# One transfer in place of four for each stored tile of dt and dt*x, and one in place of three for the rows of maxima

## The chip, the cores and the metric

The kernel runs on one core of one Trainium2 chip. The metric is the device time of one execution in microseconds (us). Before the change it is 4890.47 us, the median of three runs from 4883.07 to 4906.68 us.

## What is computed

The reference takes `L0_attn_hidden_states`, 16 sequences of 512 positions and 256 features, and passes each through six residual layers:

```
x = x + 0.5 * _L0_ffn_ref(_layernorm(x), ...)     # gated FFN, 704 wide, inputs and weights quantised in blocks of 16
x = x + _L0_attn_ref(_layernorm(x), ...)          # a state space layer ("Mamba")
x = x + 0.5 * _L0_ffn_ref(_layernorm(x), ...)
x = x + 0.5 * _L1_ffn_ref(_layernorm(x), ...)     # linear layer with 8 routed low-rank experts
x = x + _L1_attn_ref(_layernorm(x), ...)          # causal attention, 16 heads of 16, ALiBi bias
x = x + 0.5 * _L1_ffn_ref(_layernorm(x), ...)
```

Two of them matter here. The state space layer has 512 channels and 16 states per channel:

```
dt = softplus(dt_low @ W_dt + b_dt)
h  = exp(dt_t[..., None] * A) * h + (dt_t * x_t)[..., None] * B_t[:, None, :]
y  = einsum('bds,bs->bd', h, C_t)
```

The attention layer takes a softmax over scores from which the maximum of each row is subtracted first.

## The kernel before

**The stages.** Each of the 16 sequences passes through a "front" FFN, a "head" (the projections of the state space layer: convolution, dt, dt*x and the gate z), a "scan" (16 rounds of the recurrence), a "back" FFN, a first "lora" stage, "attention" and a second "lora" stage. Different sequences are in different stages at one time. On every engine a fixed table of due times (`PE_PLAN`, `DVE_PLAN`, `ACT_PLAN`, `POOL_PLAN`, `SP_PLAN`, with a period of 261.461 us) merges the stages into one list of instructions. An engine works its list off in order. So one wait holds back everything behind it on that engine, whatever stage it belongs to.

**The stores of the head.** In the head the channels are worked on in four tiles c = 0 to 3 of 128 channels by 512 positions. For each tile VectorE (DVE) writes dt (lines 1556 to 1562) and dt*x (1567), and sets the first column of dt to zero (1569). SyncE (SP) waits for that last step and issues the stores to `dt_scratch` and `dtx_scratch` in DRAM (line 572). A tile is 128 rows of 2 KB. It is stored with channels interleaved, so that later one group of four channels can be read as one run of 8 KB: in DRAM, channel 32 j + m stands in row 4 m + j. Before, that is written as four transfers of 32 rows each, one for each j. The SBUF buffers `dt` and `dtx` hold two tiles each, so tiles 0 and 2 share a buffer, and tiles 1 and 3 the other.

**Who waits for these stores.** Each buffer has a semaphore (`dt_saved[0]`, `dt_saved[1]`, the same for `dtx_saved`). These wait for them:

- ScalarE (ACT) at line 878, before it writes tile c >= 2 of dt (line 879), for the store of tile c - 2;
- DVE at line 1566, before it writes tile c >= 2 of dt*x, for the store of tile c - 2;
- DVE at line 1574, before the gate's tile m = 0 or 1 (line 1577), which takes the place of dt in the same buffer, for the store of tile 2 or 3;
- SP at lines 609 and 610, before the first load of the four rounds that read tile c;
- ACT at lines 802 and 818, before later stages write over the same memory.

TensorE's products for the gate (line 1149) wait in turn for line 1577, which frees the PSUM bank.

**The loads of the scan.** For each of 16 rounds SP issues two loads of 1024 KB, `decay` (line 616) and `state` (622). Each reads 8 rows of 8 KB and repeats each for 16 partitions. All transfers of the kernel are issued by SP on one queue.

**The rows of maxima.** In attention ACT copies the maxima, split in three bf16 parts, to `m_rows`: 12 partitions, that is 3 parts of 4 heads, of 512 elements (line 959). SP copies them into three single partitions of `qh` (line 665): one transfer for each part, 4 KB each. TensorE's scores (line 1310) wait for them, and so does the next write of `m_rows` (line 958).

Of the kernel before, what the change touches and what calls it, by code (L numbers as in the profile page):

```python
# [28 lines left out]
G = 4  # L29
J = H // G  # L30
# [6 lines left out]
Q = 4  # L37
# [48 lines left out]
def build(nc, a, out):  # L86
    with ExitStack() as ctx:
# [422 lines left out]
        def _(eng):  # L510
# [49 lines left out]
            def head(i):  # L560
                yield 31
                eng.wait_ge(head_dve.sem, head_dve.after(i, f"silu{C - 1}"))
                eng.dma_start(xs_scratch[i], xs).then_inc(xs_saved, 16)
                yield 33
                eng.wait_ge(head_act.sem, head_act.after(i, "pj"))
                eng.dma_start(bc_scratch[i], pj[RK + 1:, :]).then_inc(bc_saved, 16)
                for c in range(C):
                    yield 40 + 2.8 * c
                    eng.wait_ge(head_dve.sem, head_dve.after(i, f"zero{c}"))
                    for src, dst, done in ((dt, dt_scratch, dt_saved), (dtx_of(i), dtx_scratch, dtx_saved)):  # L570
                        for j in range(Q):
                            eng.dma_start(dst[i, c].rearrange("(q e j) l -> j (q e) l", q=Q, j=Q)[j], src[32 * j:32 * (j + 1), c % 2, :]
                                          ).then_inc(done[c % 2], 16)
                for m in range(C):
                    yield 53.7 + 2 * m
                    eng.wait_ge(head_dve.sem, head_dve.after(i, f"siluz{m}"))
                    eng.dma_start(gz_scratch[i, m], gz[:, m % 2, :]).then_inc(gz_saved[m % 2], 16)

            def scan(i):
# [23 lines left out]
                for r in range(ROUNDS):  # L603
# [4 lines left out]
                    if r % Q == 0:  # L608
                        eng.wait_ge(dt_saved[c % 2], 64 * (2 * i + c // 2 + 1))
                        eng.wait_ge(dtx_saved[c % 2], 64 * (2 * i + c // 2 + 1))  # L610

# [27 lines left out]
            def attention(r, q):  # L639
# [22 lines left out]
                def load_maxima(j):  # L662
                    eng.wait_ge(att_act.sem, att_act.after(r, f"m{j}"))
                    for w in range(3):
                        eng.dma_start(qh[MAXROW + w:MAXROW + w + 1, j % 2, :, :], m_rows[w * G:(w + 1) * G, :]).then_inc(m_loaded, 16)

# [77 lines left out]
        def _(eng):  # L744
# [52 lines left out]
            def lead(w, n, norm, q):  # L797
                p = WORK.index((w, n))
                if p >= 2 and WORK[p - 2][0] == "head":
                    yield 4.9  # L800
                    for saved in dtx_saved:
                        eng.wait_ge(saved, 128 * (WORK[p - 2][1] + 1))
                yield from hats(norm, q, xx[:, n % NX, :, :])
                if w != "head":
                    yield 10.5
                    r = FFNS.index((w, n))
                    eng.wait_ge(f.lead_dve.sem, f.lead_dve.after(r, "scaled"))
                    eng.activation(size_x[:, :], norm.hat[:, :, :].rearrange("p t d -> p (t d)"), ACT.Abs, scale=BINADE
                                   ).then_inc(f.lead_act.sem, f.lead_act.step("size"))

            def ffn(front, r, n):
# [3 lines left out]
                if heads:  # L815
                    eng.wait_ge(xs_saved, 16 * heads)
                    for b in range(2):
                        eng.wait_ge(dt_saved[b], 128 * heads)
                        eng.wait_ge(gz_saved[b], 32 * heads)
# [35 lines left out]
            def head(i):  # L855
# [18 lines left out]
                for c in range(C):  # L874
                    yield 35 + 2.8 * c
                    eng.wait_ge(head_pe.sem, head_pe.after(i, f"dt{c}"))
                    if c >= 2:
                        eng.wait_ge(dt_saved[c % 2], 64 * (2 * i + 1))
                    eng.activation(dt[:, c % 2, :], MB[(1 + c) % 2][:, :], ACT.Abs).then_inc(head_act.sem, head_act.step(f"abs{c}"))
# [57 lines left out]
            def attention(r, q):  # L937
# [16 lines left out]
                def save_maxima(j):  # L954
                    eng.wait_ge(att_pe.sem, att_pe.after(r, f"m{j}"))

                    if j or r:
                        eng.wait_ge(m_loaded, 48 * (J * r + j))
                    eng.activation(m_rows[:, :], att_bank[f"m{j}"][0:3 * G, :], ACT.Copy).then_inc(att_act.sem, att_act.step(f"m{j}"))
# [44 lines left out]
        def _(eng):  # L1004
# [243 lines left out]
            def attention(r, q):  # L1248
# [46 lines left out]
                def scores(w, j, t, g, n):  # L1295
# [4 lines left out]
                    if t == 0 and g == 0:  # L1300
                        if w == "s":
                            eng.wait_ge(qk_loaded[b], SET_LOADS * (2 * r + j // 2 + 1))
                        else:
                            eng.wait_ge(m_loaded, 48 * (J * r + j + 1))
                    for h in range(n):
# [80 lines left out]
        def _(eng):  # L1386
# [118 lines left out]
            def ffn(front, r, n):  # L1505
                small = [f.qs[:, n, :] for n in range(4)]

                def hidden(t):
                    for p, (lo, width) in enumerate(PIECES):
                        yield 21.2 + p + TILE_US * t  # L1510
                        heads = heads_before(r)
                        if t == 0 and p == 0 and heads:
                            eng.wait_ge(xs_saved, 16 * heads)
                            for b in range(2):
                                eng.wait_ge(dt_saved[b], 128 * heads)
                                eng.wait_ge(gz_saved[b], 32 * heads)
# [20 lines left out]
            def head(i):  # L1537
# [14 lines left out]
                for c in range(C):  # L1552
# [12 lines left out]
                    if c >= 2:  # L1565
                        eng.wait_ge(dtx_saved[b], 64 * (2 * i + 1))
                    eng.tensor_tensor(dtx_of(i)[:, b, :], dt[:, b, :], xs[:, c, :], ALU.mult).then_inc(head_dve.sem, head_dve.step(f"dtx{c}"))
                    eng.wait_ge(head_dve.sem, head_dve.after(i, f"dtx{c}"))
                    eng.memset(dt[:, b, 0:1], 0.0).then_inc(head_dve.sem, head_dve.step(f"zero{c}"))
                for m in range(C):  # L1570
                    yield 52.5 + 2 * m
                    eng.wait_ge(head_act.sem, head_act.after(i, f"tanhz{m}"))
                    if m < 2:
                        eng.wait_ge(dt_saved[m], 128 * (i + 1))
                    else:
# [185 lines left out]
```

## Time and profile before

| | |
|---|---|
| median of three runs | 4890.47 us |
| profiled execution, from its first to its last instruction (span) | 4905.3 us |
| PE (TensorE matmul) busy | 4033.8 us, 82% |
| DVE busy | 3994.1 us, 81% |
| ACT busy | 2371.7 us, 48% |
| POOL (GpSimd) busy | 1600.0 us, 33% |
| SP's DMA queue, time of its packets as a share of 16 engines | 64.9% |
| read from and written to HBM | 647.30 MB, 101.71 MB |

For the profiled execution the record has the span alone, with no time around it. The span is 14.8 us (0.3%) above the median of the runs and within their range. "SPq" in a row is SP's issuing of a transfer. The chain of waits is followed back from the last instruction: each piece is what released the piece after it, so the pieces fill the span. A piece "DMA a<-b" lasts from the end of the issue (or from the start of the last one) to the moment at which the waiting engine is released. A landing time is counted from issue to completion.

### The profile page before, as it was taken

What the parts mean: (1) busy time and instruction counts of PE and PEld (TensorE: products, weight loads), DVE (VectorE), ACT (ScalarE), POOL (GpSimd) and SP (SyncE); (2) the same over time, 40 slices, a digit from 0 to 9 for tenths busy, and PEclk for the clock granted to TensorE, in tenths of its full rate; (3) what the DMA queues carried; (4) which work ended last, traced back from release to release, by engine and by line L of the source; (5) the groups of instructions that cost most, each with busy time, mean ns of one, the idle gap of its engine ahead of it and who ended that gap; (6) DMA issues with size and microseconds to landing.
All of it is one profiled execution on the core that took longest, in us unless ns stands there. A gap on an engine that the chain in (4) does not pass through costs nothing.

```text
span 4905.3 us, 54168 instructions
## 1 busy us (share of the span) xinstructions
PE 4033.8 (82%) x18222; PEld 2046.2 (42%) x18251; DVE 3994.1 (81%) x5964; ACT 2371.7 (48%) x4341; POOL 1600.0 (33%) x1036
## 2 busy tenths in 40 slices
PE   4556678888989898888989898988989898786867
PEld 2223334443535354444435354444435353434343
DVE  6578889898989989898989889898989899684402
ACT  2334344555555464645555554646555554543322
POOL 0143433333334333333333333333333343332000
PEclk8778889999999999999999999999999999897867
DMA  1477668767676777777677777787677777772100
GB/s 56 118 176 180 149 170 182 174 158 185 159 171 175 163 177 175 180 166 178 158 177 178 157 176 159 177 179 180 156 176 173 159 176 161 181 174 64 42 23 28
DMA packets 241433, 753.39 MB, mean 154 GB/s; under 512 B 37650, under 2 KB 132659, under 8 KB 171524
## 3 DMA queue, kind: packets, MB, share of 16 engines
q1 hardware_dynamic: 241156, 749.95, 64.9%
q8 instruction: 144, 2.36, 0.2%
q14 instruction: 133, 1.09, 0.1%
HBM read 647.30 MB, written 101.71 MB: 153 GB/s over the span
## 4 chain that ended last, share of the span: by engine, by line
PE 47%; DVE 23%; ACT 11%; DMA 9%; issue 4%; SPq 3%; POOL 2%; ACTq 0%; DVEq 0%; POOLq 0%
PE m L1135 8%; DVE state L1608 5%; PE m L1107 5%; DVE mt L1696 4%; DMA decay<-dt_scratch 4%; DMA state<-dtx_scratch 3%; PE y L1212 2%; PE pd L1334 2%; PE m L1149 2%; DVE u L1603 2%; PE y L1201 2%; DMA dt_scratch<-front 2%; ACT shared L982 2%; PE m L1136 1%; ACT decay L912 1%
## 5 line engine op out<-in xcount | busy, mean ns | idle before, releaser
L731 POOL TENSOR_TENSOR state<-state,bc 128x1024 f32<-128x1024 f32 x512 | 1215.7, 2375 | 1764.9 <-DVE u L1603 1764.8
L1608 DVE TENSOR_TENSOR_SCAN state<-decay,u 128x1024 f32<-128x1024 f32 x512 | 1168.6, 2282 | 13.0 <-ACT decay L912 1.0
L912 ACT ACTIVATE decay<-decay,a_neg 128x511 f32<-128x511 f32 x1024 | 671.3, 712 | 268.8 <-DMA decay<-dt_scratch 268.5
L1107 PE MATMUL m<-w_gu,hats_m 128*128 128x480 f32 (+1 forms) x1536 | 699.3, 588 | 39.0 <-DVE front L1523 31.6
L1603 DVE TENSOR_TENSOR u<-state,bc 128x1024 f32<-128x1024 f32 x512 | 632.5, 1235 | 81.1 <-DMA state<-dtx_scratch 70.7
L1135 PE MATMUL m<-w_dn,front 128*128 128x256 f32 (+1 forms) x1536 | 447.7, 440 | 46.3 <-ACT front L849 46.2
L715 POOL TENSOR_TENSOR front<-front,hsc_m 128x704 f32<-128x704 f32 x128 | 205.8, 1608 | 809.8 <-DVE front L1433 809.8
L1107 PEld LDWEIGHTS m<-w_gu,hats_m 128*128 128x128 f32 x1536 | 287.7, 198 | 295.1 <-issue 215.8
L1135 PEld LDWEIGHTS m<-w_dn,front 128*128 128x128 f32 (+1 forms) x1536 | 308.1, 214 | 181.3 <-ACT front L849 89.9
L1201 PE MATMUL y<-state,sel 128*32 128x512 f32 x2048 | 288.8, 638 | 92.5 <-POOL state L731 91.3
L1149 PE MATMUL m<-hats_m,w_in 128*128 128x512 f32 x512 | 270.5, 662 | 69.1 <-DVE front L1562 38.4
L830 ACT ACTIVATE front<-m 128x240 f32<-128x240 f32 (+1 forms) x384 | 136.5, 360 | 296.4 <-PE m L1107 272.2
L1696 DVE TENSOR_REDUCE mt<-pu 128x1 f32<-128x384 f32 (+3 forms) x368 | 234.8, 638 | 46.5 <-PE pu L1313 43.0
L1696 DVE TENSOR_REDUCE mt<-pg 128x1 f32<-128x384 f32 (+3 forms) x336 | 212.5, 632 | 53.0 <-PE pg L1313 51.9
L982 ACT ACTIVATE shared<-pg 128x512 f32<-128x512 f32 (+1 forms) x384 | 215.0, 560 | 63.0 <-PE pg L1313 61.2
L853 ACT ACTIVATE xx<-m 128x256 f32<-128x256 f32 x128 | 48.9, 382 | 404.2 <-PE m L1136 404.2
L982 ACT ACTIVATE shared<-pu 128x512 f32<-128x512 f32 (+1 forms) x320 | 177.2, 554 | 90.6 <-PE pu L1313 86.6
L1056 PE MATMUL y<-minus,zero 128*128 128x512 bf16 x779 | 209.3, 401 | 0.0
L1334 PE MATMUL pd<-shared,va 128*17 128x512 f32 (+3 forms) x2048 | 199.9, 461 | 1.3
L1520 DVE SCALAR_TENSOR_TENSOR front<-front,m 128x240 f32<-128x240 f32 (+1 forms) x384 | 148.6, 387 | 59.3 <-ACT front L830 59.3
L696 POOL TENSOR_SCALAR less_r<-mv_r 128x4 f32<-128x4 f32 x48 | 13.4, 280 | 547.9 <-DVE mv_r L1484 547.9
L1308 PE MATMUL pg<-kh,shared 102*128 102x512 bf16 (+3 forms) x448 | 130.2, 332 | 73.2 <-DVE mt L1696 60.0
(264 smaller groups left out, 7177.6 us busy)
## 6 DMA issues: line engine op xcount, KB each, us to landing
decay<-dt_scratch SPq DMA_DIRECT2D x256, 1024.0 KB, 7.3
state<-dtx_scratch SPq DMA_DIRECT2D x256, 1024.0 KB, 11.5
qk_scratch<-shared SPq DMA_DIRECT2D x64, 384.0 KB, 3.1
shared<-qk_scratch SPq DMA_DIRECT2D x384, 64.0 KB
kh<-qk_scratch SPq DMA_DIRECT2D x384, 64.0 KB
xs_scratch<-front SPq DMA_DIRECT2D x16, 1024.0 KB, 5.7
dt_scratch<-front SPq DMA_DIRECT2D x256, 64.0 KB, 2.9
dtx_scratch<-hats_m SPq DMA_DIRECT2D x256, 64.0 KB, 1.9
```

The costliest lines, as they stand in the source:

```text
L731: eng.tensor_tensor(st, st, bc[:, 1:2, :].to_broadcast([P, WIDE, L]), ALU.mult).then_inc(scan_pool.sem, scan_pool.step(f"c{r}{h}"))
L912: ins = eng.activation(d, d, ACT.Exp, scale=a_neg[:, g:g + 1])
L982: eng.activation(pt[:, slot:slot + n, 0:width], heads(f"e{j}{t}{g}", width, n), ACT.Exp).then_inc(att_act.sem, att_act.step(f"e{j}{t}{g}"))
L1056: eng.matmul(bank[:, :].rearrange("p (o l) -> p o l", o=L // P), zero16[:, :], minus16[:, :].rearrange("p (o l) -> p o l", o=1).to_broadca ...
L1107: mm = eng.matmul(f.bank(f"gu{t}{p}")[:, 0:2 * width], norm.hat_t[:, k, t * P:(t + 1) * P], w_gu[:, k, 2 * lo:2 * (lo + width)], start=(k ...
L1135: eng.matmul(down[:, 0:D], f.h_t[0:rows, m, :], w_dn[0:rows, m, :], start=(m == 0), stop=False)
L1149: mm = eng.matmul(bank[:, :], w_in[:, k, m * P:(m + 1) * P], norm.hat_t[:, k, :], start=(k == 0), stop=(k == KD - 1))
L1201: mm = eng.matmul(Y[32 * j:32 * (j + 1), :], sel[:, r % Q, :], state[:, slot, j * L:(j + 1) * L], start=False, stop=(r % Q == Q - 1), skip ...
L1334: eng.matmul(PD[32 * g:32 * g + HD + 1, t * P:L], va[:, t, j * G + g, :], pt[:, (t * G + g) % NPT, 0:L - t * P], start=(t == 0), stop=True ...
L1603: eng.tensor_tensor(u[:, :].rearrange("p (j l) -> p j l", j=WIDE), st.rearrange("p (j l) -> p j l", j=WIDE), bc[:, 0:1, :].to_broadcast([P ...
L1608: eng.tensor_tensor_scan(st, decay[:, n % ND, h * WIDE * L:(h + 1) * WIDE * L], u[:, :], 0.0, ALU.mult, ALU.add).then_inc(scan_dve.sem, sc ...
L1696: eng.tensor_reduce(mt[:, t, g:g + n], heads(f"s{j}{t}{g}", (t + 1) * P, n), AX.X, ALU.max, negate=True).then_inc(att_dve.sem, att_dve.ste ...
```

## The change

For a tile, the destination keeps all its dimensions, 4 blocks (stride one row) by 32 rows (stride four rows) by 512 elements, and the source is the whole tile of 128 partitions. So one transfer of 256 KB moves what four of 64 KB moved, to the same addresses. The three copies of maxima become one, from 12 partitions to 3 partitions of 4 x 512. The values that are waited for are divided by four and by three. Nothing else is changed, and no due time.

```
                     for src, dst, done in ((dt, dt_scratch, dt_saved), (dtx_of(i), dtx_scratch, dtx_saved)):
-                        for j in range(Q):
-                            eng.dma_start(dst[i, c].rearrange("(q e j) l -> j (q e) l", q=Q, j=Q)[j], src[32 * j:32 * (j + 1), c % 2, :]
-                                          ).then_inc(done[c % 2], 16)
+                        eng.dma_start(dst[i, c].rearrange("(q e j) l -> j (q e) l", q=Q, j=Q), src[:, c % 2, :]).then_inc(done[c % 2], 16)
...
-                        eng.wait_ge(dt_saved[c % 2], 64 * (2 * i + c // 2 + 1))
-                        eng.wait_ge(dtx_saved[c % 2], 64 * (2 * i + c // 2 + 1))
+                        eng.wait_ge(dt_saved[c % 2], 16 * (2 * i + c // 2 + 1))
+                        eng.wait_ge(dtx_saved[c % 2], 16 * (2 * i + c // 2 + 1))
...
                     eng.wait_ge(att_act.sem, att_act.after(r, f"m{j}"))
-                    for w in range(3):
-                        eng.dma_start(qh[MAXROW + w:MAXROW + w + 1, j % 2, :, :], m_rows[w * G:(w + 1) * G, :]).then_inc(m_loaded, 16)
+                    eng.dma_start(qh[MAXROW:MAXROW + 3, j % 2, :, :], m_rows[:, :]).then_inc(m_loaded, 16)
...
                     if c >= 2:
-                        eng.wait_ge(dt_saved[c % 2], 64 * (2 * i + 1))
+                        eng.wait_ge(dt_saved[c % 2], 16 * (2 * i + 1))
...
                     if j or r:
-                        eng.wait_ge(m_loaded, 48 * (J * r + j))
+                        eng.wait_ge(m_loaded, 16 * (J * r + j))
...
                     if m < 2:
-                        eng.wait_ge(dt_saved[m], 128 * (i + 1))
+                        eng.wait_ge(dt_saved[m], 32 * (i + 1))
```

On SP, around the stores of the second head, stands before (a row is the line, what it writes and reads, and the destination's shape; "x4" is four in a row):

```order
L586 DMA gate<-gz_scratch 128x512
L572 DMA dt_scratch<-front 32x512 x4
L572 DMA dtx_scratch<-hats_m 32x512 x4
L572 DMA dt_scratch<-front 32x512 x4
L572 DMA dtx_scratch<-hats_m 32x512 x4
L616 DMA decay<-dt_scratch 128x1x2048
L622 DMA state<-dtx_scratch 128x1x2048
L572 DMA dt_scratch<-front 32x512 x4
L572 DMA dtx_scratch<-hats_m 32x512 x4
```

and at the same place after the change:

```order
L584 DMA gate<-gz_scratch 128x512
L571 DMA dt_scratch<-front 4x32x512
L571 DMA dtx_scratch<-hats_m 4x32x512
L571 DMA dt_scratch<-front 4x32x512
L571 DMA dtx_scratch<-hats_m 4x32x512
L614 DMA decay<-dt_scratch 128x1x2048
L620 DMA state<-dtx_scratch 128x1x2048
L571 DMA dt_scratch<-front 4x32x512
L571 DMA dtx_scratch<-hats_m 4x32x512
```

Each group of four has become one, and the destination has three dimensions, the first of size 4. The source still is 128 partitions of 512. The order of everything else is kept: the same two loads stand between the stores of tiles 1 and 2. No instruction is moved on the other engines.

## Rows read from the trace of the kernel before

**Rows 1.** Page, chain that ended last: share of the span by engine, by line.
```profile
PE 47%; DVE 23%; ACT 11%; DMA 9%; issue 4%; SPq 3%; POOL 2%; ACTq 0%; DVEq 0%; POOLq 0%
PE m L1135 8%; DVE state L1608 5%; PE m L1107 5%; DVE mt L1696 4%; DMA decay<-dt_scratch 4%; DMA state<-dtx_scratch 3%; PE y L1212 2%; PE pd L1334 2%; PE m L1149 2%; DVE u L1603 2%; PE y L1201 2%; DMA dt_scratch<-front 2%; ACT shared L982 2%; PE m L1136 1%; ACT decay L912 1%
```

**Rows 2.** Chain in order of time, first head: start us, us, what.
```profile
171.65 0.32 SPq L572
...
176.72 1.71 DMA dt_scratch<-front
...
184.78 0.07 DVE front L1569
...
189.92 1.71 DMA dt_scratch<-front
```

**Rows 3.** Timeline of ACT and DVE, first head: start, us, instruction, [idle before, releaser].
```profile
178.51 0.60 ACT L879 ACTIVATE front<-m 128x512 f32<-128x512 f32 x1 [0.47 <-DMA dt_scratch<-front]
...
190.73 0.60 ACT L901 ACTIVATE front<-m 128x512 f32<-128x512 f32 x1 [2.27 <-PE m L1149]
...
191.72 0.69 DVE L1577 SCALAR_TENSOR_TENSOR front<-front,m 128x512 f32<-128x512 f32 x1 [2.54 <-DMA dt_scratch<-front]
```

**Rows 4.** Chain in order of time, a head in mid run.
```profile
2275.88 0.51 ACT hats_r L993
...
2276.43 0.61 ACT front L879
...
2284.06 5.71 DMA dt_scratch<-front
```

**Rows 5.** Timeline of SP and DVE, the same head.
```profile
2276.99 0.53 SPq L616 DMA_DIRECT2D decay<-dt_scratch  x1
...
2282.78 1.71 SPq L572 DMA_DIRECT2D dt_scratch<-front  x4
...
2289.86 0.69 DVE L1577 SCALAR_TENSOR_TENSOR front<-front,m 128x512 f32<-128x512 f32 x1 [0.66 <-DMA dt_scratch<-front]
```

**Rows 6.** Tile dt_scratch: instructions, duration ns min/median/max; waits on it: us, times.
```profile
L572 SPq DMA_DIRECT2D dt_scratch<-front x256: 302/425/1793, 171.7 to 4202.7; - x128
L616 SPq DMA_DIRECT2D decay<-dt_scratch x256: 514/526/675, 192.8 to 4446.6; - x128
...
  ACT front L879: 20.9, 17
  DVE front L1577: 8.7, 14
```

**Rows 7.** Line L572: landing of its transfers.
```profile
DMA to landing us min/median/max: 1.6/2.2/6.3
```

**Rows 8.** Page, DMA issues: count, KB each, median us to landing.
```profile
xs_scratch<-front SPq DMA_DIRECT2D x16, 1024.0 KB, 5.7
dt_scratch<-front SPq DMA_DIRECT2D x256, 64.0 KB, 2.9
...
gz_scratch<-front SPq DMA_DIRECT2D x64, 256.0 KB, 3.1
```

**Rows 9.** Windows: window, us, busy of engines (instructions), PEclk, DMA share, GB/s.
```profile
156.00:162.00 6.00, 5.23 (x9) 1.16 (x8) 1.35 (x9) 0.68 (x1) 1.63 (x4) 0.73 0.44 178
174.00:177.00 3.00, 1.81 (x2) 0.23 (x2) 0.47 (x2) 2.22 (x3) 0.00 (x0) 0.50 0.55 142
2267.00:2270.00 3.00, 1.06 (x13) 0.42 (x13) 2.85 (x6) 2.77 (x4) 0.00 (x0) 1.00 0.95 202
2277.00:2289.00 12.00, 10.65 (x35) 3.98 (x33) 8.64 (x12) 9.64 (x15) 2.54 (x2) 0.92 0.95 224
```

**Rows 10.** Tile m_rows: its copies, and who waited: us, times.
```profile
L665 SPq DMA_DIRECT2D shared<-m_rows x192: 572/573/814, 786.0 to 4846.1; - x192
...
  PEld pu L1310: 6.8, 17
  PEld pg L1308: 1.4, 6
```

More of the change, by code:

```diff
@@ L801, in lead @@
                     for saved in dtx_saved:
-                        eng.wait_ge(saved, 128 * (WORK[p - 2][1] + 1))
+                        eng.wait_ge(saved, 32 * (WORK[p - 2][1] + 1))
                 yield from hats(norm, q, xx[:, n % NX, :, :])
@@ L817, in ffn @@
                     for b in range(2):
-                        eng.wait_ge(dt_saved[b], 128 * heads)
+                        eng.wait_ge(dt_saved[b], 32 * heads)
                         eng.wait_ge(gz_saved[b], 32 * heads)
@@ L1303, in scores @@
                         else:
-                            eng.wait_ge(m_loaded, 48 * (J * r + j + 1))
+                            eng.wait_ge(m_loaded, 16 * (J * r + j + 1))
                     for h in range(n):
@@ L1514, in hidden @@
                             for b in range(2):
-                                eng.wait_ge(dt_saved[b], 128 * heads)
+                                eng.wait_ge(dt_saved[b], 32 * heads)
                                 eng.wait_ge(gz_saved[b], 32 * heads)
@@ L1565, in head @@
                     if c >= 2:
-                        eng.wait_ge(dtx_saved[b], 64 * (2 * i + 1))
+                        eng.wait_ge(dtx_saved[b], 16 * (2 * i + 1))
                     eng.tensor_tensor(dtx_of(i)[:, b, :], dt[:, b, :], xs[:, c, :], ALU.mult).then_inc(head_dve.sem, head_dve.step(f"dtx{c}"))
```

## The prediction

> **What bounds the kernel now.** I read the chain of waits first, since no engine is busy for more than 82% of the span. By engine it is PE 47%, DVE 23%, ACT 11%, DMA 9%, SPq 3% [rows 1]. The lines that the change touches appear there as the landings of dt_scratch<-front, 2% of the span [rows 1]. In order of time the chain has 21 such pieces in 16 heads. Fifteen are of 5.2 to 5.9 us, of the kind of 2284.06 [rows 4], or 1.71 us in the first head [rows 2]: there DVE's line 1577 waits for the store of tile 2 or 3 of dt. The other six, in six heads, are mostly of 1.7 us, as that at 176.72 [rows 2], after which ACT's line 879 goes on with tile 3. So in every head the end of the kernel hangs on at least one landing of a dt store, and in six heads on two. The waits themselves look small: 20.9 us in 17 cases and 8.7 us in 14 [rows 6]. That is what the waiter lost beyond its other inputs and bounds only what faster stores could give. A store that lands later adds its lateness in full.
>
> Then SP's issues and the landings. One issue of 64 KB takes 0.425 us, and four take 1.7 us [rows 5, 6]. A 64 KB store lands after 1.6 us at the least and 2.2 us in the median over the whole line [rows 7]. Stores of 256 KB and 1024 KB whose two sides both begin with 128 rows land after 3.1 and 5.7 us [rows 8].
>
> **The change, part by part.**
>
> *Issues.* Per head 32 issues become 8. A transfer whose sides are described differently costs SP 0.526 us (decay loads) or 0.573 us (maxima) against 0.425 us for a store of matched sides [rows 6, 10]; I take 0.55. Four tiles then take SP 8 x 0.55 = 4.4 us in place of 32 x 0.47 = 15 us (0.47 is 0.425 and the gap to the next). The SP time saved is worth something only where something waits for it, which is weighed below.
>
> *How the new store is shared out.* This term decides. Before, both sides of a store begin with 32 rows, and the other large transfers begin with 128 or 16 on each side. Now DRAM begins with 4 blocks and SBUF with 128 partitions. If a transfer is cut into equal shares by the first dimension of both sides, only four shares are possible, and four of the 16 engines carry 64 KB each where they carried 4 KB of each of four transfers. No row of before shows a transfer of that size with such sides. The bounds are: all 16 engines share it, and it lands as the 256 KB row, 3.1 us; or four do. For an engine's rate I use the windows: 142 GB/s at a share of 0.55 is 142 / (16 x 0.55) = 16.1 GB/s per busy engine for stores of 2 KB rows, and 178 / (16 x 0.44) = 25.3 GB/s for the 1024 KB store [rows 9]. So 64 KB (65.5 thousand bytes) occupy an engine for 2.6 to 4.1 us. I take x = 3.3 us, the middle. Completion adds 1.6 - 0.25 = 1.35 us, the least landing less 4 KB at 16.1 GB/s [rows 7]. I choose four engines, since 4 is the only division that the first dimensions of the two sides offer.
>
> The Trainium skill speaks of this in "DMA: Bandwidth & Descriptors", section "Why a DMA increments its semaphore by 16 and not by 1": a transfer runs on k engines, k being the largest number up to 16 that divides the size of the slowest dimension above 1 on both sides. By that rule the dt and dt*x stores fall from 16 engines (32 and 32) to 4 (4 and 128), and the maxima from 4 to 3. No row of before shows it; with it the forecast below stands, without it the first rival does.
>
> *First landing, in a head like the first.* The stores of dt 0, dt*x 0 and dt 1 queue on the same four engines. Tile 1 of dt lands at 171.65 + 0.55 + 3 x 3.3 + 1.35 = 183.5, where it landed at 176.72 + 1.71 = 178.4 [rows 2]: +5.0 us (+2.9 at x = 2.6, +7.4 at 4.1), and ACT's line 879 starts that much later. From the zeroing of tile 2 (184.78) to the landing of dt 3 at 191.63 [rows 2] it took 6.85 us; now 0.55 + 9.9 + 1.35 = 11.8 us, again +5. That is +10 us in each of the six heads with two pieces on the chain: 60 us.
>
> *The other ten heads.* All engines are busy (share 0.95) with earlier loads until about 2270 [rows 9]. Then dt 0, dt*x 0 and dt 1 take 9.9 us on the four, and dt 1 lands at 2281.2. ACT took it up at 2276.43, after its line 993 at 2275.88 [rows 4]: +4.8 us. With dt*x 1 the four are free of stores at 2283.2. The two loads that stood at 2276.99 [rows 5] are now issued some 4 us earlier, but on these four engines they wait until then. Their 128 KB per engine take 5.2 us at 25.3 GB/s or 8.9 us at 224 / (16 x 0.95) = 14.7 GB/s [rows 9]. The store of dt 2, issued at 2282.78 + 4.8 = 2287.6, begins at 2288.4 to 2292.1 and lands at 2293.1 to 2296.7, where line 1577 started at 2289.86 [rows 5]: +3.2 to +6.9, the delay of ACT included. I take +4, near the lower end, since the four engines then catch up while the other twelve are idle. Ten heads give 40 us. With x = 2.6 and fast loads it is +2, with 4.1 and slow loads +11.
>
> *Dt\*x.* Line 1566 waits for the store of tile c - 2, which by the same sum is in by then. The waits of the later stages (802, 818) come tens of us after the stores. I put both at nothing, hidden by the gate's tiles.
>
> *The maxima.* Three issues of 0.573 us and two gaps become one: the rows are there 1.2 us earlier. Only 8.2 us were waited for them in 23 cases [rows 10], and no piece of the chain is such a copy. So between 0 and -8 us; I take -4. If the copy on fewer engines were slower by as much as it is issued earlier, it would be 0.
>
> **Sum.** 60 + 40 - 4 = +96 us on the profiled 4905.3, so 5001. The median stood 14.8 us below that span: 4986 us. With the low ends: 6 x 5.8 + 10 x 2 - 8 = +47. With the high ends: 6 x 14.8 + 10 x 11 = +199.
>
> **The rivals.**
>
> 1. *All 16 engines share the new store, and the time is not longer.* The least landing is then that of the 256 KB row. In the first head ACT's line 879 could start 0.47 us earlier [rows 3], then its own line 887 bounds it. Line 1577 would gain 0.4, as line 901 ends at 191.33 [rows 3]. In mid run line 1577 gains its idle 0.66 us [rows 5], then DVE's own work bounds it. That is 6 x 0.9 + 10 x 0.7 = 12 us, with the maxima up to 20: 4878 us, within 0.5%. For it speaks that the bytes and rows are the same and that the 256 KB row costs little more than one of 64 KB; against it, the first dimension of 4.
>
> 2. *The same sharing, and SP's queue was the real limit.* If what stands behind the stores on SP (the loads of the next rounds) also comes out earlier to use, three quarters of the store issues on the chain go. In the six heads ten to twelve issues of 0.47 stand there in a row: about 50 us, so -38, with the maxima -46: 4845 us. Against it: where the loads stand right behind the stores [rows 5], no piece of the chain waits for these loads. It decides from the point at which a landing of 256 KB takes less than four issues and a landing of 64 KB (1.4 + 2.2 = 3.6 us).
> The Trainium skill pleads for this side too: its page "DMA: Bandwidth & Descriptors", section "Rules for kernel authors", would merge small transfers into one large, since those of 64 KB pay mostly overhead. The rows of 2.2 and 3.1 us agree for matched sides.
>
> 3. *Four engines, but the work beside it hides them.* With x = 2.6, and DVE and ACT finding other work in order, only the six heads lose, some 3 us each: +20, 4910 us.
>
> 4. *Four engines, and SP is held up.* Single issues already took up to 1.79 us, four times the median [rows 6]. A deep queue on four engines could stop SP, so that the loads for the other twelve wait too. Then the scan's loads come about two transfers (6 us) later in each of 16 heads: 96 us more, 5082 us.
>
> **How the numbers follow.** A measurement of this kernel tells about 0.5% (24 us) from no change. The forecast (four engines, +47 to +199 us) has 0.77, rival 4 has 0.10, rival 3 has 0.05, rival 1 has 0.05, rival 2 has 0.03. Rival 3 and nearly all of rival 1 are within 0.5%: same 0.09. Faster is 0.04, slower 0.87. The range leaves out rivals 1 and 2 and the outermost part of the forecast and of rival 4: 4915 to 5075 us.
>
> **What would show it.** Right: line 571 has 64 issues each of dt and dt*x at about 0.55 us with a median landing of 5 to 9 us; the idle time of ACT's dt line and of the gate's line on DVE for dt_scratch grows from 30 us to over 80 us; the chain's share of dt_scratch landings grows from 2% to 3 or 4%; the DMA share falls to about a quarter while only stores run. Wrong on the sharing: a landing near 3.1 us, and a time within 20 us of before. Wrong on the cover: landings of 5 us or more, and no growth of the chain's pieces. Rival 4: issues on SP of 2 us and more, and later decay and state loads in the head. The copies of maxima should show 64 issues of about 0.57 us and no more waits than before.

## The result, and the profile after

The changed kernel takes 4942.1 us, the median of four runs from 4936.15 to 4945.4. The kernel before takes 4891.32 us on the same chip, the median of four from 4883.07 to 4906.68. The ratio is 1.009, with a 95% interval of 1.0066 to 1.0113: 51 us slower. The forecast was 4986 us, 95 us slower. The direction and the sharing over four engines came out as forecast; the forecast loss is 1.9 times the measured one.

The page has a span of 4943.6 us, 38.3 us more than before, with the same work: PE 4041.4 us busy, DVE 3993.8, ACT 2372.6. The mean granted TensorE clock is 0.914 (before 0.915), and PE is busy for 7.6 us more than before. In later runs on another chip the clock is 0.907 to 0.913 in six runs of the changed kernel (median 0.911) and 0.909 to 0.920 in 18 of the kernel before (median 0.917). So a lower clock goes with the late landings; what it adds to the loss was not separated. The chain by engine and by line, beside [rows 1]:

```profile
PE 45%; DVE 24%; ACT 12%; DMA 11%; issue 4%; POOL 2%; SPq 1%; ACTq 0%; DVEq 0%; POOLq 0%
PE m L1132 8%; PE m L1104 5%; DVE state L1605 5%; DVE mt L1693 4%; DMA dt_scratch<-front 4%; DMA decay<-dt_scratch 4%; DMA state<-dtx_scratch 3%; PE m L1146 2%; PE y L1209 2%; DVE u L1600 2%; PE y L1198 2%; PE pd L1331 2%; ACT decay L909 2%; PE m L1133 2%; ACT shared L979 1%
```

SP's issues fall from 3% to 1%, and DMA rises from 9% to 11%: the landings of dt_scratch alone go from 2% to 4% of the span (90.2 us in 21 pieces before, 202.8 us in 25 pieces now). SP time was saved and paid for in landing time.

The two tiles, with the durations in ns (min/median/max) and who waited (us, times), beside [rows 6, 10]:

```profile
L614 SPq DMA_DIRECT2D decay<-dt_scratch x256: 514/521/817, 197.2 to 4501.1; - x128
L571 SPq DMA_DIRECT2D dt_scratch<-front x64: 502/508/650, 171.9 to 4249.2; - x64
...
  ACT front L876: 93.0, 32
  DVE front L1574: 14.0, 13
```

```profile
L662 SPq DMA_DIRECT2D shared<-m_rows x64: 698/779/869, 806.5 to 4885.2; - x64
...
  PEld pu L1307: 6.9, 17
  PEld pg L1305: 1.2, 6
```

ACT now waits 93.0 us where it waited 20.9, and in all 32 of its cases. DVE's gate line has 14.0 us in place of 8.7. That inequality is the key to the size: the first landing of a head hurts in every head, the second hardly anywhere. The copy of maxima takes SP 0.78 us, not the 0.57 I took, but one copy stands where three and their gaps took 1.8 us; the waits of PE for it are unchanged.

The first head, in the chain (start us, us, what), beside [rows 2]:

```profile
174.82 8.53 DMA dt_scratch<-front
...
192.69 8.44 DMA dt_scratch<-front
```

and in the timelines of ACT and of DVE (start, us, instruction, idle before and its releaser), beside [rows 3]:

```profile
178.29 0.60 ACT L876 ACTIVATE front<-m 128x512 f32<-128x512 f32 x1 [8.62 <-DMA dt_scratch<-front]
183.43 0.60 ACT L876 ACTIVATE front<-m 128x512 f32<-128x512 f32 x1 [1.85 <-DMA dt_scratch<-front]
```

```profile
189.70 0.06 DVE L1566 MEMSET front<- 128x1 f32 x1
...
196.03 0.69 DVE L1574 SCALAR_TENSOR_TENSOR front<-front,m 128x512 f32<-128x512 f32 x1 [3.37 <-DMA dt_scratch<-front]
201.22 0.69 DVE L1574 SCALAR_TENSOR_TENSOR front<-front,m 128x512 f32<-128x512 f32 x1 [4.50 <-DMA dt_scratch<-front]
```

Tile 1 lands just before 183.43, where 183.5 was forecast and 178.4 was before. Line 1574 starts with tile 1 of the gate at 201.22, where it stood at 191.72: +9.5 us. In this head the forecast's "+5 and again +5" holds.

The windows of this head, in which little but these stores runs (window, us, busy of PE, PEld, DVE, ACT, POOL, then PEclk, DMA share, GB/s), beside [rows 9]:

```profile
175.00:178.00 3.00, 1.07 (x2) 0.00 (x0) 0.00 (x0) 0.00 (x0) 0.00 (x0) 0.50 0.26 89
178.00:181.00 3.00, 0.00 (x0) 0.00 (x0) 0.00 (x0) 2.65 (x4) 0.00 (x0) 0.50 0.26 101
181.00:184.00 3.00, 0.00 (x0) 0.00 (x0) 0.69 (x1) 1.15 (x2) 0.00 (x0) 0.50 0.27 103
```

A share of 0.26 is 4.2 of 16 engines for nine microseconds: four engines carry the stores. The completions that the trace records say the same: each merged store raises its semaphore in five steps, for tile 0 of this head one at 172.98, 1.1 us after the issue, and four at 177.41 to 178.21, when the data are in. Each store of 64 KB before has 16 steps, all at its landing. The four engines move 101 GB/s, 24 GB/s for each, so 64 KB take 2.7 us. Here the trace agrees with the Trainium skill, "DMA: Bandwidth & Descriptors", section "Why a DMA increments its semaphore by 16 and not by 1": a transfer runs on the largest number of engines, up to 16, that divides the slowest dimension above 1 of both its sides, here 4 and 128.

The head in mid run, in the chain, on SP and on DVE, beside [rows 4, 5]:

```profile
2303.39 8.91 DMA dt_scratch<-front
```

```profile
2300.48 0.60 SPq L571 DMA_DIRECT2D dt_scratch<-front  x1
...
2307.75 0.56 SPq L614 DMA_DIRECT2D decay<-dt_scratch  x1
...
2318.73 0.55 SPq L571 DMA_DIRECT2D dt_scratch<-front  x1
```

```profile
2325.68 0.69 DVE L1574 SCALAR_TENSOR_TENSOR front<-front,m 128x512 f32<-128x512 f32 x1 [0.53 <-DMA dt_scratch<-front]
```

The store of tile 2 reaches line 1574 in 2325.68 - 2318.73 = 7.0 us. Before it was 2289.86 - 2282.78 = 7.1 us. The second store is on four engines and no later than before. Why is seen in the windows of this stretch:

```profile
2311.00:2315.00 4.00, 0.00 (x0) 0.00 (x0) 0.00 (x0) 2.54 (x4) 0.00 (x0) 0.81 1.05 273
2318.00:2321.00 3.00, 3.00 (x4) 1.26 (x5) 2.85 (x6) 0.49 (x1) 0.00 (x0) 0.50 0.26 90
```

Before, the store was issued at 2282.78 into the two loads of the scan (share 0.95 over the stretch [rows 9]). Now it is issued when they have ended: the share is 0.26, the store has its four engines alone. It pays for four engines and no longer for the loads. (The granted clock of 0.50, that is 1.2 GHz, follows a stretch in which PE did nothing: it is busy for 0.00 of 4 us from 2311 on.)

It is much the same in all 15 heads after the first. The second store comes 5.8 to 6.2 us after the last decay load in the kernel before and 7.7 to 11.5 us after it in the changed kernel. Line 1577 (now 1574) starts 6.5 to 7.3 us after the issue of that store before, and 6.3 to 7.3 us now. In nine of these heads the share in the first 3 us after the issue is 0.25 to 0.48, in the other six the loads still run (0.82 to 1.00) but are further on.

**Where the 51 us lie.** DVE executes the same 5964 instructions in the same order in both traces, so each can be matched with its partner. Three marks in each head cut the time: the zeroing of tile 0 (line 1566, before 1569), the zeroing of tile 2, and the last tile of the gate (line 1574, before 1577). The first part holds the wait for the first landings, the second that for the landings of tiles 2 and 3.

| growth against before, us | heads 0, 1, 2, 4, 7, 15 | other ten heads | all |
|---|---|---|---|
| first part | 25.1 | 28.8 | 53.9 |
| second part | 2.4 (4.2 of it in head 0) | 0.1 | 2.5 |
| between heads | | | -7.2 |
| after the last head | | | -10.2 |

The heads 0, 1, 2, 4, 7 and 15 are the prediction's "six heads with two pieces". The chain of before has two pieces in five of them only. In head 7 it has the first, and behind it goes on through TensorE's products for the gate:

```profile
2002.72 1.71 DMA dt_scratch<-front
...
2010.03 6.73 PE m L1149 x8
```

The parts give +39.0 us; the last instruction of DVE stands 38.7 us later than before, the rest being rounding. The -10.2 at the end is not the change's: the same piece is 5.3 to 19.5 us shorter than in the profile of before in every kernel run below, and the span of before stands 14.0 us above its median time, that of after 1.5 us above its own. Without it, 53.9 + 2.5 - 7.2 = 49.2 us remain, close to the 51 of the medians.

### The profile page after: what moved, and what is told of

The parts are those of the page before. It is cut to its first block, busy times and chain, and to the rows that moved or that the text cites. A ratio compares the mean times of both kernels' runs of the same rounds, so it can differ in the third digit from the quotient of the medians.

```text
span 4943.6 us, 53656 instructions
## 1 busy us (share of the span) xinstructions
PE 4041.4 (82%) x18222; PEld 2053.1 (42%) x18251; DVE 3993.8 (81%) x5964; ACT 2372.6 (48%) x4341; POOL 1598.3 (32%) x1036
## 4 chain that ended last, share of the span: by engine, by line
PE 45%; DVE 24%; ACT 12%; DMA 11%; issue 4%; POOL 2%; SPq 1%; ACTq 0%; DVEq 0%; POOLq 0%
PE m L1132 8%; PE m L1104 5%; DVE state L1605 5%; DVE mt L1693 4%; DMA dt_scratch<-front 4%; DMA decay<-dt_scratch 4%; DMA state<-dtx_scratch 3%; PE m L1146 2%; PE y L1209 2%; DVE u L1600 2%; PE y L1198 2%; PE pd L1331 2%; ACT decay L909 2%; PE m L1133 2%; ACT shared L979 1%
## 5 line engine op out<-in xcount | busy, mean ns | idle before, releaser
L1600 DVE TENSOR_TENSOR u<-state,bc 128x1024 f32<-128x1024 f32 x512 | 632.5, 1235 | 68.3 <-DMA state<-dtx_scratch 57.8
L1146 PE MATMUL m<-hats_m,w_in 128*128 128x512 f32 x512 | 284.8, 696 | 107.7 <-DVE front L1559 81.7
L1146 PEld LDWEIGHTS m<-hats_m,w_in 128*128 128x128 f32 x512 | 104.1, 220 | 253.5 <-issue 104.6
L846 ACT ACTIVATE front<-m 128x512 f32<-128x512 f32 (+1 forms) x256 | 119.5, 487 | 143.1 <-PE m L1125 140.3
## 6 DMA issues: line engine op xcount, KB each, us to landing
state<-dtx_scratch SPq DMA_DIRECT2D x256, 1024.0 KB, 11.6
```

The costliest lines, as they stand in the source:

```text
L1146: mm = eng.matmul(bank[:, :], w_in[:, k, m * P:(m + 1) * P], norm.hat_t[:, k, :], start=(k == 0), stop=(k == KD - 1))
L1600: eng.tensor_tensor(u[:, :].rearrange("p (j l) -> p j l", j=WIDE), st.rearrange("p (j l) -> p j l", j=WIDE), bc[:, 0:1, :].to_broadcast([P ...
```

## The experiments

Each time is a median, and the ratio is against the kernel before on the same chip, with its 95% interval. Growth is that of the table above, summed over 16 heads: first part / second part, us.

| kernel | us | ratio | interval | growth |
|---|---|---|---|---|
| changed kernel, again | 4946.65 | 1.0087 | 1.0056 to 1.0118 | 53.2 / 8.6 |
| maxima only | 4882.33 | 0.9974 | 0.9954 to 0.9994 | 3.3 / 4.1 |
| stores only | 4949.58 | 1.0102 | 1.0076 to 1.0127 | 53.3 / 9.3 |
| one transfer, plain rows | 4864.04 | 0.9933 | 0.9907 to 0.9959 | -15.3 / -8.6 |
| one transfer, 16 blocks | 4874.65 | 0.9943 | 0.9920 to 0.9966 | -14.7 / -8.8 |
| one transfer, 8 blocks | 4888.18 | 0.9988 | 0.9969 to 1.0007 | -1.1 / 8.4 |
| natural order, same result | 4871.73 | 0.9954 | 0.9937 to 0.9971 | -19.7 / -9.7 |
| only dt merged | 4954.15 | 1.0107 | 1.0089 to 1.0125 | 57.8 / 3.9 |
| only dt*x merged | 4903.01 | 1.0008 | 0.9995 to 1.0020 | 15.7 / 2.0 |
| only tiles 0 and 1 merged | 4940.79 | 1.0078 | 1.0049 to 1.0107 | 54.8 / -3.2 |
| only tiles 2 and 3 merged | 4928.16 | 1.0057 | 1.0035 to 1.0080 | -8.1 / 43.0 |

All but "stores only" have the merged copy of the maxima, so 0.9974 is what their other edits are to be held against. The growth is that of one execution each, and uncertain by several us: it is 7.4 us in "maxima only", where no store is changed, and 56.4 and 61.8 in two profiles of the changed kernel.

**Which of the two edits.** The first kernel has the copies of maxima merged and the stores as before, the second the stores merged and the copies as before.

```
# maxima only: line 571 as before
for j in range(Q):
    eng.dma_start(dst[i, c].rearrange("(q e j) l -> j (q e) l", q=Q, j=Q)[j], src[32 * j:32 * (j + 1), c % 2, :]).then_inc(done[c % 2], 16)
# stores only: line 662 as before
for w in range(3):
    eng.dma_start(qh[MAXROW + w:MAXROW + w + 1, j % 2, :, :], m_rows[w * G:(w + 1) * G, :]).then_inc(m_loaded, 16)
```

> The kernel before with the three copies of maxima made one, the stores of dt and dt*x left as four each. Theory (the loss comes from the dt stores alone, each carried by four of the 16 engines): the time of before within 0.2%, since the new copy takes SP 0.78 us in place of three of 0.573 us and TensorE waited as long for the rows as before (6.9 and 1.2 us in the changed kernel, 6.8 and 1.4 us before). Rival (the maxima bring the 10 us that the changed kernel gains back near its end): 5 to 10 us faster than before. Rival (they carry part of the loss): slower than before by 10 us or more.

> The changed kernel with the three copies of maxima put back: only the stores are merged. Theory: the ratio of the changed kernel to before, 1.007 to 1.011, some 40 to 50 us slower than before. Rival (the maxima share in the loss): under 1.005.

The stores alone are 1.0102, the whole loss. The maxima alone are 0.9974, 13 us faster with an interval of 3 to 23 us: more than the 4 us of the forecast, and more than the 0.2% expected before this run. No piece of the chain and no wait in the profile holds these 13 us, so their place stays open. The two edits would add to 1.0076, and the whole was measured at 1.009 and 1.0087, within the intervals.

**Is it the first dimension?** Three kernels keep one transfer of 256 KB and SP's one issue, and change only how the destination in DRAM is described: all 128 rows in order, 16 blocks of 8 rows, 8 blocks of 16 rows. In all three the channels stand in another order than the loads of the scan take them for, so their output is not the reference's.

```
-  eng.dma_start(dst[i, c].rearrange("(q e j) l -> j (q e) l", q=Q, j=Q), src[:, c % 2, :])
+  eng.dma_start(dst[i, c], src[:, c % 2, :])                                  # plain rows
+  eng.dma_start(dst[i, c].rearrange("(b a) l -> a b l", a=16), src[:, c % 2, :])   # 16 blocks
+  eng.dma_start(dst[i, c].rearrange("(b a) l -> a b l", a=8), src[:, c % 2, :])    # 8 blocks
```

> The changed kernel, but a tile is stored in plain order, so that both sides of the transfer are 128 rows of 512. The channels in DRAM are then in another order than the loads take them for: this leaves out the interleaving, and the output is not the reference's. Size, number and place of the transfers are those of the changed kernel. Theory (four engines carry a store because its sides begin with 4 and 128): all 16 carry it, it lands about 3 us after its issue as the gate's store of 256 KB does, ACT's waits for dt_scratch fall from 93 us to below those of before (20.9 us), and the time is 0 to 20 us below before (4871 to 4891). Rival (a store of 256 KB is slow as such, or SP's shorter issue lets the loads run into the stores): the time stays within 15 us of the changed kernel's 4942.

> The changed kernel, but the destination is 16 blocks by 8 rows in place of 4 blocks by 32: the same bytes, as many dimensions, rows as scattered. The channels in DRAM are in another order than the loads take them for, so the output is not the reference's. Theory (the first dimension of both sides sets the number of engines, here 16 and 128, so 16 engines): as with plain rows, 0 to 20 us below before; what is left of the late landing is the start of a transfer with such a description. In the changed kernel a first store landed 6.3 us after its issue, of which 2.6 us are data at 25 GB/s per engine, so some 3 us are not data; here it should land after 3.5 to 4 us. Rival (the three-dimensional description is slow to start or to carry out, whatever its first dimension): the landing stays at 5 us or more and the time above 4920.

> The changed kernel with the destination as 8 blocks by 16 rows (the channels in DRAM in another order than the loads take them for, so the output is not the reference's). Theory (eight engines carry it, 32 KB each, 1.3 us at 25 GB/s): a first store lands after 4 to 5 us, between 16 blocks and 4 blocks, the second tile is in some 7.4 us after the first was issued, nearly as early as before the change (6.8), so the time is within 10 us of sixteen blocks: ratio 0.994 to 0.999. The DMA share while only stores run is 0.5 in place of 0.26. Rival (landing does not follow the number of engines): as with 4 blocks, 1.008, or exactly as with 16.

The windows of the first head, with 16 blocks and then with 8:

```profile
172.00:175.00 3.00, 2.16 (x3) 0.49 (x2) 2.74 (x6) 0.00 (x0) 0.00 (x0) 0.50 0.55 163
175.00:178.00 3.00, 1.19 (x2) 0.00 (x0) 0.00 (x0) 2.89 (x4) 0.00 (x0) 0.50 0.61 185
178.00:181.00 3.00, 0.00 (x0) 0.00 (x0) 0.69 (x1) 2.92 (x5) 0.00 (x0) 0.50 0.00 1
```

```profile
175.00:178.00 3.00, 1.20 (x2) 0.00 (x0) 0.00 (x0) 1.71 (x2) 0.00 (x0) 0.50 0.51 173
```

Eight blocks give a share of 0.51, that is 8 engines. Sixteen blocks rise above what eight engines could show and are done by 178, where four blocks ran until 184. The steps of the semaphore agree: nine for a store with 8 blocks (eight and the early one), and 16 with 16 blocks and with plain rows. And the time follows: 0.9943, 0.9988 and 1.009 for 16, 8 and 4 blocks. A destination of three dimensions as such costs nothing (16 blocks against plain rows: 0.9943 and 0.9933). So the loss is the count of engines, shown by changing that count alone. One transfer on all 16 engines even gains: 0.9933 and 0.9943 against 0.9974, 15 to 20 us, and first and second part are some 15 and 9 us shorter than before. With 8 blocks the merging neither gains nor loses. Two expectations were off in size: plain rows and 16 blocks came 35 and 25 us below before, where 0 to 20 us were expected (13 us of it belong to the maxima), and 8 blocks stand 0.0045 above 16 blocks, some 22 us, where 10 were expected.

**A version that is right and faster.** The interleaving can be moved from the stores to other transfers. This kernel stores plain rows, so that a group of the scan is four neighbouring channels, and what meets the scan's output (gate, skip, W_out, A_log and D) is loaded with its rows in the interleaved order, as four transfers of 32 rows each.

```
+  eng.dma_start(dst[i, c], src[:, c % 2, :]).then_inc(done[c % 2], 16)
+  for j in range(Q):
+      eng.dma_start(gate[32 * j:32 * (j + 1), n % 2, :], gz_scratch[i, c].rearrange("(m j) l -> j m l", j=Q)[j]).then_inc(gate_loaded[n % 2], 16)
...
+  g = (j * C + r // Q) * Q + r % Q
```

> A version that computes the whole reference: tiles are stored in plain order by one transfer of matched sides (128x512), the maxima by one, and the scan takes the channels in the order in which they then stand. For that the loads of skip and gate, W_out, D and A_log are taken in permuted rows, by four transfers of 32 rows each in place of one. Theory: the stores are carried by 16 engines, and the 20 added issues per sequence (16 for gate, 4 for skip, less the 5 they replace) are for data that nothing waits for, so the time is that of plain rows within 10 us, ratio to before 0.991 to 0.997. Rival (what was won lay in SP's queue, and the added issues give it back): ratio 0.998 to 1.003.

It computes what the reference asks and takes 4871.73 us, 0.9954 [0.9937, 0.9971] of before: faster than both kernels. Of this, 0.9974 is what the maxima alone give; the 0.0020 beyond is within the two intervals. Its store of dt costs SP 0.32 us, and the waits for it fall:

```profile
L574 SPq DMA_DIRECT2D dt_scratch<-front x64: 319/320/347, 173.0 to 4174.5; - x64
...
  ACT front L881: 15.5, 11
  DVE front L1579: 4.8, 9
```

**Which of the two streams.** One kernel merges only dt, one only dt*x.

```
# only dt merged; the other kernel has "is dtx_saved"
if done is dt_saved:
    eng.dma_start(dst[i, c].rearrange("(q e j) l -> j (q e) l", q=Q, j=Q), src[:, c % 2, :]).then_inc(done[c % 2], 16)
else:
    for j in range(Q): ...   # four transfers
```

> The changed kernel with the stores of dt merged and those of dt*x four again. Theory (each merged dt store lands late by itself, and also queues behind the dt*x stores on four engines): about two thirds of the loss stay. A tile's dt lands some 6 us after its issue as in the changed kernel, but the second tile no longer stands behind 64 KB of dt*x per engine, so ACT's delay is 2 to 3 us per head in place of 3.4; ratio to before with the merged maxima 1.003 to 1.007. Rival (SP's queue sets the second landing): with five more issues between the two, 1.009 and more.

> The changed kernel with the stores of dt*x merged and those of dt four again. Nothing on the chain waits for dt*x itself. Theory: dt's second tile stands behind 64 KB per engine of dt*x on four engines, 2.6 us, part of it hidden: the delay is 0 to 1.5 us per head, ratio to before 0.996 to 1.002. Rival (the loss comes from the traffic on four engines in general, both stores alike): half of the loss, 1.004 to 1.006.

The second came as expected, the first did not: dt alone costs the full 1.0107, where 1.003 to 1.007 were expected and the rival (SP's queue sets the second landing) had 1.009 and more. So the loss does not need dt to queue behind dt*x on the same four engines. A merged store of dt is late by itself (ACT's line 881 starts at 178.28, 6.8 us after the issue at 171.53), and the four issues of dt*x behind it take SP longer. In the first head that longer queue costs nothing that can be seen: dt 1 is issued at 175.59 (174.82 in the changed kernel) and ACT takes it up at 183.16 (183.43). For the other heads the rival is not excluded. SP's queue in the first head, with dt merged and then with dt*x merged:

```profile
171.53 0.65 SPq L572 DMA_DIRECT2D dt_scratch<-front  x1
172.23 3.31 SPq L575 DMA_DIRECT2D dtx_scratch<-hats_m  x4
175.59 0.56 SPq L572 DMA_DIRECT2D dt_scratch<-front  x1
176.19 4.15 SPq L575 DMA_DIRECT2D dtx_scratch<-hats_m  x4
```

```profile
173.03 1.73 SPq L575 DMA_DIRECT2D dt_scratch<-front  x4
174.80 0.65 SPq L572 DMA_DIRECT2D dtx_scratch<-hats_m  x1
175.93 3.37 SPq L575 DMA_DIRECT2D dt_scratch<-front  x4
```

Four issues that come behind a merged store take 3.3 to 4.2 us, and 1.7 us where none is ahead of them. It is one or two of the four that are long, 1.2 to 1.9 us; the others take 0.3 to 0.7 us. That is the forecast's rival 4 on a small scale. In the changed kernel itself it hardly arises: no issue of a store is longer than 0.91 us. In "only dt*x merged" it completes the issue of dt 1 at 179.30 and not at 177.6; The 15.7 us of the first part can come from this, or, as expected before the run, from dt 1 standing behind dt*x 0 on the same four engines; no run separates the two.

**Which landing.** Two kernels merge the stores (dt and dt*x) of tiles 0 and 1 alone, or of tiles 2 and 3 alone.

```
if c < 2:        # the other kernel has c >= 2
    eng.dma_start(dst[i, c].rearrange("(q e j) l -> j (q e) l", q=Q, j=Q), src[:, c % 2, :]).then_inc(done[c % 2], 16)
else:
    for j in range(Q): ...   # four transfers
```

> The changed kernel with one transfer per tile for tiles 0 and 1 only; tiles 2 and 3 are stored by four again. Theory (the cost lies in the landing before ACT's write of tiles 2 and 3, which waits for tiles 0 and 1): nearly the whole loss, ratio to before 1.006 to 1.010, with 2 to 5 us per head between the zeroing of tile 0 and that of tile 2, and nothing after it. The step of the prediction as recorded: only the first of two landings is late, so the six heads with two pieces lose 5 us and not 10, and half of the loss is gone.

> The changed kernel with one transfer per tile for tiles 2 and 3 only. Theory: a late landing of tile 2 or 3 costs almost nothing, except some 4 us in the first head, where no loads and no other stage lie beside it: in later heads the wait for it was already filled, before by the scan's loads ahead of the store, now by the store itself. Ratio to before 0.997 to 1.000. The step of the prediction as recorded: 5 us in each of six heads and up to 4 in the others, 30 us and more, ratio 1.004 or above.

> The changed kernel itself, beside the two halves on the same chip. Both theories: 1.007 to 1.011 of before. Tiles 0 and 1 alone should account for at least four fifths of that by the theory, for half by the step as recorded.

The changed kernel gave 1.0087 again, beside these two on one chip. The first pair alone is 1.0078, as expected, and its growth lies wholly in the first part: 54.8 us. The last pair alone missed my theory: it costs 1.0057, with 43.0 us of growth, in the second part. Over "maxima only" (0.9974) the pairs cost 0.0104 and 0.0083; added up that would be 1.0161, and both together were measured at 1.009 and 1.0087. The late landing of tiles 2 and 3 is a real cost where the first pair is on time, and is nearly gone where the first pair is late. SP, then DVE, in the mid-run head with the last pair alone:

```profile
2295.39 0.52 SPq L619 DMA_DIRECT2D decay<-dt_scratch  x1
...
2301.22 0.60 SPq L572 DMA_DIRECT2D dt_scratch<-front  x1
```

```profile
2310.05 0.69 DVE L1579 SCALAR_TENSOR_TENSOR front<-front,m 128x512 f32<-128x512 f32 x1 [2.41 <-DMA dt_scratch<-front]
```

```profile
2301.00:2304.00 3.00, 2.08 (x6) 0.77 (x5) 2.82 (x6) 1.59 (x3) 0.00 (x0) 1.00 1.00 213
2304.00:2307.00 3.00, 3.00 (x11) 0.99 (x10) 2.93 (x3) 2.52 (x5) 1.60 (x1) 1.00 0.75 166
```

Here the store of tile 2 comes 5.8 us after the first load of the scan, as before, is issued into busy engines (share 1.00) and reaches line 1579 after 8.8 us, 1.8 more than the 7.1 of before. In the changed kernel it comes 11.0 us after that load (2307.75 to 2318.73), the engines are empty, and it takes 7.0 us. The loads do not wait for the first pair: SP issues them when DVE's scan has set their buffer free. So the delay of the first part moves the second store out of the loads' way.

## Why the size of the prediction was wrong

**Right: four engines.** The share of 0.26, the four late steps of the semaphore, and the order 16, 8, 4 blocks show it.

**Right: the first landing.** Forecast at 183.5 us, and ACT took it up at 183.43. Two errors met in it. The data go faster than I took (2.7 us for 64 KB, not 3.3), and there is more around them: 183.4 - 171.9 - 3 x 2.7 = 3.4 us where I took 0.55 + 1.35 = 1.9. In the six heads of this term the first landing was forecast at +5.0 each, 30 us, and the first part grew by 25.1.

**Wrong, and the step that failed: "From the zeroing of tile 2 ... now 0.55 + 9.9 + 1.35 = 11.8 us, again +5. That is +10 us in each of the six heads with two pieces on the chain: 60 us."** The second +5 came in head 0 alone: its second part grew by 4.2 us, and those of the other five by -1.8 us together. I read 184.78 to 191.63 in the first head, where no load of the scan is under way, and carried it to five heads in which loads stood before the second store (share 1.02 in the 3 us after its issue, 0.42 in the first head). In four of them the old piece of 5.2 to 5.9 us was the loads' and not the stores'. In the fifth, head 7, the chain has no second piece at all: by its own rule the sum should have had 55 us and not 60. Lateness of the first landing does not add to the wait for the second: it replaces it. "Only tiles 2 and 3" shows that the cost is there (43.0 us), "only tiles 0 and 1" shows that the first pair alone already makes the growth of both (54.8 us in the first part, against 53.9), and the changed kernel that they do not add. The six heads give 27.5 us in place of 60.

**Mis-sized: the other ten heads.** They were taken at +4, 40 us in all, and are 28.9. The cover by the loads was seen there ("+4, near the lower end"). What was missed is that in heads 3, 5, 9, 10, 11 and 13 the first part grows by 1.8 to 2.2 us only. ACT works in order, and in those heads PE held it up before, for 2.3 to 2.7 us at line 993, which stands just ahead of the dt line. Head 13, before and then after:

```profile
3646.31 0.60 ACT L993 ACTIVATE hats_r<-pg 128x512 f32<-128x512 f32 x1 [2.67 <-PE pg L1368]
```

```profile
3690.96 0.60 ACT L876 ACTIVATE front<-m 128x512 f32<-128x512 f32 x1 [2.64 <-DMA dt_scratch<-front]
```

A wait of 2.67 us for PE became one of 2.64 us for the store, one line further on in ACT's list: that much of the lateness cost nothing. This could be seen in the trace of before, head by head; the prediction took one head for ten.

**Wrong, without weight: when the loads are issued.** "Now issued some 4 us earlier" held SP's queue for their limit. From the first store of the head to the first load it is 2307.75 - 2300.48 = 7.3 us, and was 2276.99 - 2268.85 = 8.1: 0.9 us earlier. DVE's scan sets them free.

**Terms not in the sum.** Between heads 7.2 us come back. That later work fills in there is a guess: in the other kernels this part lies between -11.6 and +3.1 us, and in "maxima only" at -0.6. The maxima brought 13 us alone, where I took 4.

So 100 us of growth in the heads were forecast, and 56.4 came. Of the missing 44 us, 28 are the second landings of the six heads (5 of them that of head 7, which had no place in the sum), 5 their first, and 11 the ten other heads.

**The rivals.** That all 16 engines share the store is excluded by the shares. That the work beside it hides all (rival 3, 4910 us) is excluded by the time, but its mechanism is what failed my step: half of the lateness was hidden. That SP is held up (rival 4) was seen only where small issues stand behind a merged store, and these are gone in the changed kernel. That SP's queue was the real limit (rival 2): with all engines and the issues saved the stores gain 15 to 20 us over "maxima only", well under the 38 of that rival.

## What to carry to other kernels

Before merging transfers, look at the first dimension of both sides, and keep it a multiple of 16: the same 256 KB in one transfer were 0.3 to 0.4% faster than four transfers with all 16 engines (0.9933 and 0.9943 against 0.9974), and 1.0 to 1.2% slower with four (1.0102; 1.009 against 0.9974). The Trainium skill, "DMA: Bandwidth & Descriptors", section "Rules for kernel authors", asks to merge small transfers ("under 64 KB you're paying mostly overhead"), and in another row to use all 16 engines by an outermost dimension that is a multiple of 16. The runs here agree with the first only where the second is kept. When a delay is counted at two waits in a row, ask for the second what the wait was made of before: if a third party (here the loads) set it and does not move, the first delay is taken out of the second and not added.

## What the runs showed of the hardware

- A store on four engines takes longer than its data at the full rate ask for: ACT took up tile 0 of the first head 178.29 - 171.92 = 6.4 us after its issue, 3.7 us of it besides the 2.7 us of data. With 16 blocks it was 3.0 us (172.03 to 175.05). The packets in the two traces begin alike, 1.3 us after the issue (173.20 and 173.29). But on four engines the first 16 of the 128 rows take up to 0.9 us each and the last of them ends at 175.1; most of the later ones take 0.08 us each. Why the first rows are slow was not settled.
- SP's issues of 64 KB are slower behind a store on four engines: 0.83 to 1.04 us in the mean of four (single ones up to 1.87 us in the first head), against 0.43 us.
- A store of 256 KB of dt costs SP 0.32 us with plain rows on both sides, 0.51 us with 4 blocks, 0.52 us with 16 and 0.57 us with 8; that of dt*x right behind it costs 0.43, 0.58, 0.60 and 0.57 us.
- One copy of the maxima to three partitions takes SP 0.78 us, and one to a single partition 0.57 us.
